# Moving a reciprocal and its multiply two reductions earlier in VectorE's order

## The reference, cut to what matters

```
q = LN(x) @ Wq.T + bq;  k = ctx @ Wk.T + bk;  v = ctx @ Wv.T + bv
scores = q k^T / sqrt(8);  attn = softmax(scores)      # per batch and head, 56 x 1500
x = x + tanh(g_xattn) * ((attn @ v) @ Wo.T + bo)
x = x + tanh(g_ffn) * moe(LN(x))                       # 160 experts, top 8, and a shared one
```

## Time and profile before

| what | value |
|---|---|
| median of three runs | 1217.17 us (1213.94 to 1219.04) |
| the profiled execution, its own time | 1221.3 us |
| its span, first to last instruction | 1219.8 us |
| PE busy | 1111.6 us, 91% |
| VectorE busy | 979.9 us, 80% |
| ScalarE busy | 837.2 us, 69% |
| GpSimd busy | 600.3 us, 49% |
| mean granted TensorE clock | 0.971 |

### The profile page before, as it was taken

One profiled execution on the slowest core, in us unless ns is written; L12 is line 12 of the kernel. 1 busy time (PEld: TensorE's weight loads), 2 busy tenths in 40 slices (PEclk: granted clock), 3 DMA queues, 4 the chain that ended last, 5 costly groups with the idle time before them and its releaser, 6 DMA issues.

```text
span 1219.8 us, 37798 instructions
## 1 busy us (share of the span) xinstructions
PE 1111.6 (91%) x12090; PEld 708.3 (58%) x12090; DVE 979.9 (80%) x1680; ACT 837.2 (69%) x1790; POOL 600.3 (49%) x1011
## 2 busy tenths in 40 slices
PE   1586999999999999999999998876999999999998
PEld 0254666666666666666766666653555555555554
DVE  2775778778787787787787787746999999999998
ACT  1353666666666666666666666564888888888887
POOL 7895688878878877878888773000000000000000
PEclk9987999999999999999999999867999999999999
DMA  8769679779789797787897862114677676766764
GB/s 135 161 129 157 135 138 165 142 152 153 141 162 151 141 161 140 155 155 141 160 144 142 168 116 66 42 34 126 216 235 225 229 236 231 225 236 234 225 229 129
DMA packets 200998, 197.04 MB, mean 162 GB/s; under 512 B 161183, under 2 KB 167391, under 8 KB 200966
## 3 DMA queue, kind: packets, MB, share of 16 engines
q1 hardware_dynamic: 189446, 175.64, 65.2%
q0 software_dynamic: 11520, 20.99, 6.4%
HBM read 109.96 MB, written 12.55 MB: 100 GB/s over the span
## 4 chain that ended last, share of the span: by engine, by line
PE 71%; DVE 12%; ACT 5%; issue 4%; SPq 3%; DMA 3%; POOL 1%; ACTq 0%; DVEq 0%; POOLq 0%
PE bank L1228 14%; PE bank L1256 14%; PE bank L1081 11%; PE bank L1067 11%; PE bank L1098 7%; PE bank L1134 6%; ACT p_exp L640 4%; DVE rec L936 4%; PE bank L1122 3%; DVE part_max L838 3%; DMA ctT<-ctx_parts 2%; DVE o_nrm L940 1%; PE bank L1153 1%; PE bank L1146 1%; SPq L354 1%
## 5 line engine op out<-in xcount | busy, mean ns | idle before, releaser
L640 ACT ACTIVATE p_exp<-bank 125x448 f32<-125x448 f32 x768 | 389.5, 546 | 260.7 <-PE bank L1081 260.5
L838 DVE TENSOR_REDUCE part_max<-bank 128x1 f32<-128x500 f32 x672 | 422.5, 671 | 127.4 <-PE bank L1098 123.8
L1081 PE MATMUL bank<-q_st,k_stk 97*125 97x224 f16 x1536 | 286.3, 272 | 20.4 <-ACT p_exp L640 6.3
L1098 PE MATMUL bank<-kparts,q_blk 128*128 128x500 f16 x672 | 256.8, 384 | 10.8 <-DVE part_max L838 7.3
L1081 PEld LDWEIGHTS bank<-q_st,k_stk 97*125 97x125 f16 x1536 | 187.1, 140 | 127.2 <-ACT p_exp L640 73.9
L1256 PE MATMUL bank<-ctT,w_ring 128*128 128x448 f16 x960 | 234.0, 353 | 3.1 <-DVE ctT L978 3.1
L732 ACT ACTIVATE ctT<-bank 128x448 f32<-128x448 f32 x320 | 173.7, 543 | 40.6 <-PE bank L1228 16.1
L978 DVE TENSOR_TENSOR ctT<-k_stk,ctT 128x448 f16<-128x448 f32 x320 | 197.8, 618 | 0.3 <-ACT ctT L738 0.2
L1067 PE MATMUL bank<-p_exp,v_sb 125*25 125x168 f32 (+1 forms) x6144 | 191.8, 267 | 0.6 <-ACT p_exp L640 0.6
L738 ACT ACTIVATE ctT<-k_stk 128x448 f16<-128x448 f32 x320 | 181.7, 568 | 3.6 <-DVE k_stk L972 3.5
L1228 PE MATMUL bank<-q_hi,w_ring 128*128 128x448 f16 x640 | 174.9, 355 | 1.9 <-ACT k_stk L720 1.9
(11 more groups left out here) (139 smaller groups left out, 1231.7 us busy)
## 6 DMA issues: line engine op xcount, KB each, us to landing
v_sb<-c_scratch SPq DMA_DIRECT2D x114, 448.0 KB, 3.8
k_stk<-kparts SPq DMA_DIRECT2D x384, 93.8 KB, 4.8
ctx_in<-in_ctx_dram SPq DMA_DIRECT2D x31, 750.0 KB
k_stk<-c_scratch SPq DMA_DIRECT2D x38, 448.0 KB, 4.0
w_scratch<-w_out POOLq DMA_DIRECT2D x80, 128.0 KB, 6.6
w_in<-in_L_ffn_w_gate_dram POOLq DMA_DIRECT2D x160, 32.0 KB, 4.4
w_in<-in_L_ffn_w_down_dram POOLq DMA_DIRECT2D x80, 64.0 KB, 8.0
v_sb<-c_scratch SPq DMA_DIRECT2D x6, 336.0 KB, 5.3
```

What stands on the lines that cost most here:

```text
L640: act.activation(p_exp[0:KP, j % PR, f * 448:(f + 1) * 448], ST[f][0:KP, 0:448], ACT.Exp).then_inc(exp_done, 1)
L838: v.reduce_max(part_max[:, i // NCH, i % NCH:i % NCH + 1], SM[i % NSM][:, 0:CK], axis=AX.X).then_inc(sm_maxed, 1)
L1081: last = pe.matmul(ST[f][0:KP, (g % 2) * GC:(g % 2 + 1) * GC], k_stk[0:97, u, g, j * KP:(j + 1) * KP], q_st[0:97, u, g, :, :].rearrange("p ...
L1098: pe.matmul(SM[i % NSM][:, 0:CK], rows, kparts[:, u, 0, c * CK:(c + 1) * CK], start=True, stop=True).then_inc(sm_done, 1)
```

## The change

The two statements of the division become a function `normalise`, and the call moves from `evacuate(step, 5)`, which runs at place 6 behind reductions 12 and 13, to place 5 behind reductions 10 and 11 (and behind `evacuate(step, 4)`, which holds nothing). No instruction is added or removed, and no wait. PE's, ScalarE's, GpSimd's and SyncE's programs are the same. In step 32 VectorE also evicts transposed tokens (L874, L875) at place 5; the division now comes ahead of them.

```diff
@@ body(step) of VectorE
                         v.tensor_copy(o_raw[:, :], OB[:, 0:OC]).then_inc(o_copied, 1)
+                    if on(step, 3) and k == SPREAD_AT:
+                        normalise(step)
                     if on(step, 1) and k == NEG_AT - 1:
...
@@ the end of evacuate(step, k)
-                if on(step, 3) and k == SPREAD_AT:
-                    h, u = back(step, 3)
-                    b = num((h, u))
-                    dve.wait_ge(spread_done, b + 1)
-                    until(dve, nrm_done, b)
-                    v.reciprocal(rec[:, :], VB[:, 0:OC]).then_inc(rec_done, 1)
-                    dve.wait_ge(rec_done, b + 1)
-                    if u == 0:
-                        until(dve, op_done, h)
-                    v.tensor_tensor(o_nrm[:, :, u, :], rec[:, :].rearrange("p (n t) -> p n t", t=T),
-                                    o_raw[:, :].rearrange("p (n t) -> p n t", t=T), ALU.mult).then_inc(nrm_done, 1)
+            def normalise(step):
+                h, u = back(step, 3)
+                b = num((h, u))
+                dve.wait_ge(spread_done, b + 1)
+                until(dve, nrm_done, b)
+                v.reciprocal(rec[:, :], VB[:, 0:OC]).then_inc(rec_done, 1)
...
```

More of the change, by code:

```diff
@@ L930, in evacuate @@
                                                op0=ALU.add, op1=ALU.subtract).then_inc(k_lo_done, 1)
-                if on(step, 3) and k == SPREAD_AT:
-                    h, u = back(step, 3)
-                    b = num((h, u))
-                    dve.wait_ge(spread_done, b + 1)
-                    until(dve, nrm_done, b)
-                    v.reciprocal(rec[:, :], VB[:, 0:OC]).then_inc(rec_done, 1)
-                    dve.wait_ge(rec_done, b + 1)
-                    if u == 0:
-                        until(dve, op_done, h)
-                    v.tensor_tensor(o_nrm[:, :, u, :], rec[:, :].rearrange("p (n t) -> p n t", t=T),
-                                    o_raw[:, :].rearrange("p (n t) -> p n t", t=T), ALU.mult).then_inc(nrm_done, 1)
+            def normalise(step):
[4 more added lines that the diff above has]
+                v.reciprocal(rec[:, :], VB[:, 0:OC]).then_inc(rec_done, 1)
+                dve.wait_ge(rec_done, b + 1)
+                if u == 0:
+                    until(dve, op_done, h)
+                v.tensor_tensor(o_nrm[:, :, u, :], rec[:, :].rearrange("p (n t) -> p n t", t=T),
+                                o_raw[:, :].rearrange("p (n t) -> p n t", t=T), ALU.mult).then_inc(nrm_done, 1)
             attention(dve, body)
```

## The result

The changed kernel takes 1200.41 us (median of 4, 1198.87 to 1205.85), beside 1216.97 for the kernel before (4 runs): ratio 0.9863, 95% interval 0.9826 to 0.9900. A second group of runs gave 1198.70 beside 1218.43, ratio 0.9842 (0.9807 to 0.9877). Forecast were 1203 and a gain of 14.3 us; it is 16.6 in the first group and 19.7 in the second.

A forecast was written before the change was run, and what follows sets the result against it. PE's own order was taken to bound the attention stage, with one VectorE-made hole per step. 22.7 us with o_nrm always free, less 7.5 and 0.9 for holding by GpSimd, gave 14.3 and 1203 us; range 1194 to 1213.

The forecast's parts named there:

- The bound: Attention stage: PE's own order bounds it, with one VectorE-made hole per step; waits for o_nrm total 20.0 us.
- The free step: Steps with o_nrm unheld: values start 3.64 us after the spread matmul's start, 0.65 earlier; reduction 12 has 0.02 to spare.
- The lock: o_nrm with two SBUF inputs and GpSimd's SBUF reads exclude each other; takes 7.5 and 0.9 us off 22.7.
- the seven late steps: Steps 11, 13, 15, 17, 23, 25, 27, where L499 starts later: o_nrm taken as free, gain 0.97 us each.
- The close call: In seven odd steps from 11 to 27, o_nrm starts ahead of GpSimd's L499 by only 0.08 us.
- The ten steps alike: Steps 8, 10, 12, 14, 16, 18, 22, 24, 26, 28: L499 leads by 0.26, values 0.10 us later.
- the forecast's picture: Step 18 and its like: L499 first by 0.26 us, o_nrm ends at +3.53, values start at +4.39.
- The end of the stage: Step 32, where the division also passes two token evictions: gain 0.65 us, bounds 0 and 1.9.
- Both kinds caught: Rival: GpSimd wins in the seven late steps too, each losing 0.12; gain 6.7 us, 1210.5; chance 0.20.
- nothing caught: Rival: GpSimd never holds o_nrm at the new place; gain 22.7 us, 1194.5; chance 0.16.
- Given back: Rival: another chain through the loop was just as late; change under 0.5%, say 1216; chance 0.10.
- Slower by a second loss to L574: Rival: o_nrm stands behind L499, in odd steps also L574, delaying matmul 15; 13 us slower, 1230; chance 0.08.

The follow-up runs named there:

- the kernel with step 32 alone: The kernel before, with the division moved in step 32 only; one execution, 29.65 us from spread 32 to spread 33, 31.71 before.
- The form with one PSUM input: The changed kernel with the reciprocal written back into bank 6 in PSUM, so o_nrm has one SBUF input; 1192.55 us, ratio 0.9801 to before.
- the doubled reciprocal: The changed kernel with the reciprocal in bank 6 and a second, unused reciprocal of the same size ahead; 1240.84 us, ratio 1.0170 to before.
- the two experiments: Reciprocal written back into bank 6, in the kernel before (1215.70 us, ratio 0.9971) and in the changed kernel (1192.55 us, ratio 0.9801).

## Why the prediction was right

**The bound.** Right. From spread 3 to spread 31 it became 15.8 us shorter in the profile, and the offsets account for it: their sum over steps 3 to 30 fell by 16.2, the stretch from the values of step 4 to spread 5 grew by 1.0 (22.04 to 23.08), and all other such stretches shrank by 0.02 each, 0.6 in all. The 1.0 is not the change's: that stretch took 21.54 in the second profile of the changed kernel, and 20.49 in the kernel with step 32 alone, whose program is that of before up to step 31.

**The free step.** Right: +3.65 against +3.64, with reduction 12 just in time. The form with one PSUM input shows it in 29 of 29 steps, and the doubled reciprocal shows that the 0.86 carries on where there is no slack.

**The lock.** Its mechanism was right: taken away at either place, it gives back what the durations said (4.0 and 5.9 us in the sum of offsets). In the seven late steps 6.1 us were gained, forecast 6.9, but by luck in part. The close call, o_nrm just ahead of L499, came about in three of them (15, 17 and 27, by 0.10 to 0.11 us), and o_nrm was first each time. In the four others GpSimd was at another place of its order. In 11 and 23 it was issuing a DMA from L458, and o_nrm took its 0.39; in 13 and 25 it was issuing one from L460, and o_nrm was held to +4.0. Step 13, GpSimd and then VectorE:

```profile
338.10 0.71 POOL L460 DMA_DIRECT2D w_in<-in_L_ffn_w_down_dram  x1
338.81 0.70 POOL L497 CAST ctx_parts<-ctx_in 128x512 f16<-128x512 f32 x1
...
338.28 0.77 DVE L942 TENSOR_TENSOR o_nrm<-rec,o_raw 128x224 f32<-128x224 f32 x1
```

o_nrm ended 0.24 after the DMA issue and well ahead of the end of L497, so the issue held it, which the forecast did not have among the holders. It was there to be seen before: in steps 9, 19 and 29 of that kernel o_nrm took 0.69 and ended 0.23 after L460. Issues of L458 did not hold it: in this profile six o_nrm started with 0.47 us or more of one still to run and took 0.39. With one input in PSUM no issue of L460 held o_nrm either: in step 13 of the changed kernel's form 0.43 us of one were left, and it took 0.39. Why L460 holds and L458 does not stays open.

**The ten steps alike.** This is the term that was mis-sized. Each was to lose 0.10, 1.0 us together; they gained 1.6. I had read from the trace of before that GpSimd's wait for PE sets the phase anew every second step, and had put the loss of its room at nothing. The wait sets the phase only while GpSimd has that room. An issue of a DMA of GpSimd stalls for 2.35 us, here in step 9 and in the kernel before at the same place, and how GpSimd comes back shows in its waits ahead of q_blk:

```profile
254.14 0.72 POOL L460 DMA_DIRECT2D w_in<-in_L_ffn_w_down_dram  x1 [2.35 <-issue]
...
300.75 1.68 POOL L551 TENSOR_TENSOR q_blk<-q_hi,head_mask 128x896 f16<-128x896 f16 x1 [0.56 <-PE bank L1100]
...
344.32 1.68 POOL L551 TENSOR_TENSOR q_blk<-q_hi,head_mask 128x896 f16<-128x896 f16 x1 [1.51 <-PE bank L1100]
...
388.18 1.68 POOL L551 TENSOR_TENSOR q_blk<-q_hi,head_mask 128x896 f16<-128x896 f16 x1 [2.20 <-PE bank L1100]
```

With shorter steps it needs some 100 us to be back in phase (step 14), where before it needed 50 (a wait of 3.13 us at 305); until then L499 is late and o_nrm is ahead of it. Steps 14, 16 and 26 had the forecast's picture (+4.39 to +4.41), 18 and 28 a worse one (+4.64, +4.50), the five others start at +3.64 to +3.99. So the lock took 5.9 us of the 22.8 by which the offsets of before exceed the free 105.7, not the forecast's 8.4.

The stall is not alone. GpSimd also waits ahead of L497 for a DMA, the transposes of its context parts, from 200 to 720 us; the kernel before, the changed kernel, and one such wait:

```profile
POOL ctx_parts L497 <- DMA ctT<-ctx_parts: 0.4, 1, 0.4
...
POOL ctx_parts L497 <- DMA ctT<-ctx_parts: 6.1, 7, 1.7
...
433.89 0.61 POOL L497 CAST ctx_parts<-ctx_in 128x512 f16<-128x512 f32 x1 [0.19 <-DMA ctT<-ctx_parts]
```

That wait puts L499 of step 18 at +2.36 in place of +2.11, just ahead of o_nrm, which is then held longest. And step 8, at +3.99, lies ahead of the stall in step 9. That these two delays unsettle the phase is read from the trace; no run took either away.

**The end of the stage.** The forecast took 0.65 for step 32, which was right for the wait, and nothing for the clock, which is 1.4 us more. The two profiled spans are 22.2 us apart: spread 3 came 1.3 later, and then 15.8, 0.7 (step 31), 2.1 and, between spreads 33 and 34, 5.0 were gained. The 1.3 is not the change's, for in its second profile spread 3 came at 112.54, with 112.82 before. Nor can the 5.0 be counted for it, for the changed kernel took 16.55 us between spreads 33 and 34 in one profile and 20.71 in the next. Whether the change makes the short outcome more frequent stays open: of the ten profiles the four with a clock of 0.80 behind step 32 took 19.2 to 21.6 us there; of the six with 1.00 four took 16.6 to 16.8 and two 20.5 to 20.7. The medians, 16.6 and 19.7 us apart, are the measure of the change. The forecast's 14.3, plus 2.5 for the lock and 1.4 for the clock, makes 18.2, between them.

**The rivals.** Both kinds caught, and nothing caught: neither, the truth lay between the forecast and the latter. Given back: nothing that comes again from one profile to the next. Slower by a second loss to L574: the longest o_nrm is 1.39, the whole of one L499 and no more.

## What to carry to other kernels

Ask of a wait what hangs behind the waiting work, not only when it ends: the same division sets PE at its end plus 0.15 in one place and plus 0.86 in another, so of the 1.37 us by which it ends earlier the move pays 0.66 at most. When a small instruction's duration varies between two neighbours' positions, look at the other engine at that moment; if it has two SBUF inputs, try to give it one from PSUM, which here costs nothing and is worth 5.9 us in the sum of offsets behind the move and 4.0 without it (6.2 and 2.7 in the medians). A phase between two engines that was read from a trace is good only while the engine whose wait resets it keeps its room.

## What the hardware showed that I had not expected

The o_nrm with one input in PSUM takes as long as with both in SBUF (391 to 393 ns against 391 to 394 where nothing holds it), and a reciprocal can write over its own input in PSUM in nearly the same time (median 1.556 us for 1.547). The Trainium skill, page "SBUF — State Buffer", section "Who interferes with whom", says that a VectorE instruction with at most one SBUF input, outside the two-port modes, does not contend with GpSimd; the two experiments agree, with no duration over 0.39 us in the 32 of each.

In the last steps of the attention stage TensorE's granted clock falls to half for stretches of varying length in one and the same kernel. From spread 33 to spread 34, whose work is fixed, in the first profile of the changed kernel and in the second:

```profile
783.90:800.45 16.55, 13.85 (x226) 10.24 (x223) 9.12 (x22) 12.49 (x25) 0.00 (x0) 0.97 0.18 50
```

```profile
780.95:801.65 20.70, 18.66 (x226) 13.47 (x223) 9.12 (x22) 12.59 (x25) 0.00 (x0) 0.66 0.14 40
```

PE stood for 4.42 us ahead of this in both, for two table loads and a sigmoid on ScalarE. What decides which of the two it is stays open.
